# A first batch that takes its maxima straight from fp32 projections, context padded to 128 rows, and new instruction orders

## The reference

```python
xn = layernorm(x)
q, k, v = heads(xn @ Wq + bq), heads(xn @ Wk + bk), heads(xn @ Wv + bv)
y  = softmax(causal(q @ k.T / sqrt(8))) @ v                  # self attention
qc, kc, vc = heads(xn @ Wcq + bcq), heads(ctx @ Wck + bck), heads(ctx @ Wcv + bcv)
y += softmax(qc @ kc.T / sqrt(8)) @ vc                       # cross attention
x  = x + tanh(g_xattn) * (y @ Wp + bp)
# routed feed-forward, 16 experts, 4 of them per token, from 2 of 4 groups
xn = layernorm(x)
combine = route(sigmoid(xn @ router_weight.T), router_bias)  # 2.5 x normalised weights
x  = x + tanh(g_ffn) * sum_e combine[:, e] * ((silu(xn @ gate_e.T) * (xn @ up_e.T)) @ down_e.T)
```

## Time and profile before

| | |
|---|---|
| median of 3 runs | 371.14 us (369.06 to 373.66) |
| profiled execution | 365.4 us, of which the traced span is 363.7 us |
| TensorE busy | 331.4 us (91%), 3186 matmul instructions |
| VectorE busy | 258.0 us (71%) |
| ScalarE busy | 195.8 us (54%) |
| GpSimd busy | 151.6 us (42%) |
| chain that ended last | TensorE 77%, VectorE 6%, DMA 5%, SP's issuing 4% |

### The profile page before, as it was taken

One profiled execution on the slowest core, in us unless ns is written; L12 is line 12 of the kernel. 1 busy time (PEld: TensorE's weight loads), 2 busy tenths in 40 slices (PEclk: granted clock), 3 DMA queues, 4 the chain that ended last, 5 costly groups with the idle time before them and its releaser, 6 DMA issues.

```text
span 363.7 us, 8615 instructions
## 1 busy us (share of the span) xinstructions
PE 331.4 (91%) x3186; PEld 243.1 (67%) x3186; DVE 258.0 (71%) x637; ACT 195.8 (54%) x399; POOL 151.6 (42%) x174
## 2 busy tenths in 40 slices
PE   0576899989999997999999999999999999989797
PEld 0343365666677675778877778777778796766665
DVE  3423585877889889887857786977888786556751
ACT  1232156747766774576565854677457555643131
POOL 8452343304225438416750459226700280712414
PEclk9999999999999999999999999999999999999999
DMA  5474543665644564045724344417412501405000
GB/s 138 79 165 151 165 123 103 190 203 175 153 125 132 154 152 132 24 150 139 187 76 132 92 112 137 145 49 167 127 50 99 119 2 50 85 4 131 2 14 14
DMA packets 32505, 40.45 MB, mean 111 GB/s; under 512 B 3056, under 2 KB 29440, under 8 KB 29984
## 3 DMA queue, kind: packets, MB, share of 16 engines
q1 hardware_dynamic: 32464, 39.91, 41.6%
HBM read 29.84 MB, written 7.45 MB: 103 GB/s over the span
## 4 chain that ended last, share of the span: by engine, by line
PE 77%; DVE 6%; DMA 5%; SPq 4%; issue 3%; POOL 2%; ACT 2%; POOLq 0%; ACTq 0%; DVEq 0%
PE bank L818 14%; PE bank L884 13%; PE bank L777 8%; PE bank L799 8%; PE bank L905 6%; PE bank L774 6%; PE bank L796 5%; PE bank L838 2%; DMA k_stack<-part_scr 2%; DMA comb<-c_scr 2%; SPq L478 2%; PE bank L859 2%; DVE row_max L969 2%; PE bank L840 1%; PE bank L825 1%
## 5 line engine op out<-in xcount | busy, mean ns | idle before, releaser
L969 DVE TENSOR_REDUCE row_max<-bank 128x2 f32<-128x512 f32 (+1 forms) x224 | 148.2, 685 | 49.8 <-PE bank L777 32.8
L689 ACT ACTIVATE probs<-bank 128x512 f32<-128x512 f32 x224 | 127.9, 595 | 60.6 <-PE bank L799 35.3
L884 PE MATMUL bank<-xn2T,w_pairs_sb 128*128 128x256 f32 x256 | 66.4, 386 | 1.5 <-issue 1.1
L818 PE MATMUL bank<-probs,v_ext 128*32 128x256 f32 (+1 forms) x1024 | 61.8, 362 | 0.0
L613 POOL TENSOR_TENSOR f_h<-f_h,comb 128x512 f32<-128x512 f32 x32 | 40.1, 1270 | 28.9 <-ACT comb L710 12.1
L777 PE MATMUL bank<-k_stack,q_stack 72*128 72x256 bf16 x256 | 49.4, 291 | 2.5 <-DVE row_max L969 1.5
L884 PEld LDWEIGHTS bank<-xn2T,w_pairs_sb 128*128 128x128 f32 x256 | 44.0, 190 | 8.3 <-issue 3.1
L799 PE MATMUL bank<-q_stack,k_stack 73*128 73x256 bf16 x256 | 47.3, 282 | 0.3 <-ACT probs L689 0.2
L406 POOL TENSOR_TENSOR rest<-proj,part 128x512 f32<-128x512 f32 x14 | 16.2, 1155 | 68.0 <-ACT part L662 68.0
L818 PEld LDWEIGHTS bank<-probs,v_ext 128*32 128x32 f32 x1024 | 27.1, 110 | 21.9 <-issue 7.2
L774 PE MATMUL bank<-k_stack,q_stack 121*128 121x128 bf16 (+1 forms) x384 | 38.4, 229 | 2.3 <-DVE row_max L969 2.0
(11 more groups left out here) (111 smaller groups left out, 372.5 us busy)
## 6 DMA issues: line engine op xcount, KB each, us to landing
q_stack<-part_scr SPq DMA_DIRECT2D x45, 192.0 KB
k_stack<-part_scr SPq DMA_DIRECT2D x45, 192.0 KB
comb<-c_scr SPq DMA_DIRECT2D x14, 512.0 KB, 6.4
part_scr<-part SPq DMA_DIRECT2D x48, 128.0 KB, 2.2
x_in<-in_x SPq DMA_DIRECT2D x8, 128.0 KB, 2.6
w_pairs_sb<-in_w_pairs SPq DMA_DIRECT2D x1, 1024.0 KB, 8.0
out<-y_out SPq DMA_DIRECT2D x8, 128.0 KB, 2.8
q_stack<-q_stack SPq DMA_DIRECT2D x2, 384.0 KB, 5.5
```

The costliest lines, as they stand in the source:

```text
L689: nc.scalar.activation(probs[:, seq % NP, :], exp_bank[s % 2][:, :], ACT.Exp).then_inc(exp_done, 1)
L818: last = pe.matmul(pv_bank[32 * n:32 * n + VW, col + q0:col + T], v_ext[:, b % 2, kind, kt].rearrange("p h v -> p (h v)")[:, at:at + VW], ...
L884: last = pe.matmul(bank_of[:, n * T:(n + 1) * T], w[:, e0:e0 + 128], xn2T[:, :], start=True, stop=True)
L969: nc.vector.tensor_reduce(row_max[:, kind, qt, h0:h0 + nh], max_bank[k % 2][:, :].rearrange("p (h k) -> p h k", h=nh), AX.X, ALU.max).then ...
```

## The change

- The maxima of batch 0 no longer come from the stack. The weights of the four projections are copied with columns in order of heads (wh), the projections are computed a second time with them (hp), and the keys are copied four times, each time with all but every fourth head's rows multiplied by zero (hk, with of_head), the queries once (hq). Head h is then a product over a set of 32 rows (h // 4): first_max (word mxd) computes two chunks at a time, whose heads lie in different sets of 32 rows, in two PSUM banks, with the banks of the experts as the second pair. S1_CHUNKS is reordered for that. The stack of batch 0 is still made, for the exponentials; its waits move there.
- Context and its weights are padded with zeros to 128 rows by two memsets on VectorE.
- GpSimd's constants (more) and the clearing of v_ext (vclear) wait for the first normalisation; rstd1:0 stands ahead of more.
- All six orders are new. Among others: both cross splits of batches 0 and 1 are on GpSimd, which were on VectorE; batch 1's maxima follow xnT:2; SP loads batch 2 ahead of the masks, and the second half of batch 0's cross keys comes after the stores of batch 1.

```diff
-S1_CHUNKS = [(CROSS, qt, H // 2 * half + 2 * g, 2, 256) for half in range(2) for qt in range(NQ) for g in range(4)]
+S1_CHUNKS = [(CROSS, qt, H // 2 * half + 2 * g, 2, 256) for half in range(2) for qt in range(NQ) for g in (0, 2, 1, 3)]
 CROSS_C1 = len(S1_CHUNKS)
-S1_CHUNKS += [(SELF, 0, 4 * g, 4, 128) for g in range(4)] + [(SELF, 1, 2 * g, 2, 256) for g in range(8)]
+S1_CHUNKS += [(SELF, 0, 4 * g, 4, 128) for g in range(4)] + [(SELF, 1, 2 * g, 2, 256) for g in (0, 2, 1, 3, 4, 6, 5, 7)]
...
     'pe': '''
-        xnT:0 proj:0 proj:0:1 vproj:0 xnT:1 proj:1 proj:1:1 vproj:1 max:0 max:0:1 xnT:2 max:0:2 max:0:3 proj:2 max:0:4
-        max:0:5 max:0:6 max:0:7 max:0:8 max:0:9 max:0:10 proj:2:1 max:0:11 max:0:12 shift:0 max:0:13 max:0:14 max:0:15
...
+        xnT:0 colh:0 proj:0 hp:0 hp:0:1 proj:0:1 mxd:0 mxd:0:1 mxd:0:2 mxd:0:3 vproj:0 mxd:0:4 shift:0 xnT:1 proj:1
+        mxd:0:5 hp:0:2 mxd:0:6 hp:0:3 exp:0 mxd:0:7 mxd:0:8 exp:0:1 mxd:0:9 shift:0:2 exp:0:2 mxd:0:10 exp:0:3
+        proj:1:1 mxd:0:11 exp:0:4 exp:0:5 mxd:0:12 mxd:0:13 pv:0 exp:0:6 shift:0:1 exp:0:7 vproj:1 exp:0:8 exp:0:9
+        pv:0:1 xnT:2 max:1 exp:0:10 max:1:1 exp:0:11 max:1:2 proj:2 max:1:3 max:1:4 exp:0:12 max:1:5 max:1:6 exp:0:13
+        exp:0:14 max:1:7 proj:2:1 max:1:8 exp:0:15 max:1:9 pv:0:2 pv:0:3 max:1:10 exp:0:16 exp:0:17 max:1:11 max:1:12
...
     'pool': '''
-        more:0 rstd1:0 vclear:0 rstd1:1 xn1:1 sp1:0:1 sp3:0:1 rstd1:2 xn1:2 sp1:1:1 xres:0 sp3:1:1 sp1:2 sp3:2 sp1:2:1
...
+        rstd1:0 more:0 xres:0 sp1:0 sp3:0 vclear:0 rstd1:1 xn1:1 sp1:0:1 sp3:0:1 sp1:1 sp3:1 sp1:1:1 sp3:1:1 rstd1:2
...
     'sp': '''
-        load:0 w:0 load:1 tri:0 pd0:0 load:2 pd2:0 pd1:0 tri:0:1 pd0:0:1 kh:0 qh:0 kh:0:1 pd2:1 ones:0 pd1:0:1 pd2:0:1
-        pd0:1 pd1:1 qh:0:1 qst:0:1 kst:0:1 pd0:1:1 pd1:1:1 shd:0 pd2:1:1 kst:1 shd:0:2 qst:1 pd0:2:1 load:3 pd0:2
...
+        load:0 w:0 load:1 load:2 tri:0 pd1:0 pd0:0 pd2:0 ones:0 tri:0:1 kh:0 qh:0 load:3 shd:0 qh:0:1 pd1:0:1 pd0:1
+        pd1:1 pd2:0:1 pd2:1 pd0:0:1 kh:0:1 shd:0:2 kst:1 qst:1 shd:0:1 pd0:1:1 pd2:1:1 kst:0:1 pd1:1:1 qst:0:1 qst:1:1
...
-        w_ctx_sb = sb("w_ctx_sb", [CC, 2 * C])
+        w_ctx_sb = sb("w_ctx_sb", [C, 2 * C])
...
-        ctx_in = sb("ctx_in", [CC, NX, T])
+        ctx_in = sb("ctx_in", [C, NX, T])
...
+        first_banks = (max_bank, (gate_bank, up_bank))
...
             def more_constants():
+                pool.wait_ge(xn_done, 1)
...
             def clear_values():
+                pool.wait_ge(xn_done, 1)
...
+            def by_head(kind, n):
+
+                act.wait_ge(of_head_made, 3)
+                act.wait_ge(heads_ready, (2, 1)[n > 0] if kind == CROSS else 3)
+                q, k = (exp_bank[1][:, 0:T], exp_bank[0][:, 0:T]) if kind == CROSS else (pv_bank[:, T:2 * T], pv_bank[:, 0:T])
+                if n == 0:
+                    last = nc.scalar.activation(q_h[kind], q, ACT.Identity, bias=bias_qh[:, 1 - kind:2 - kind], scale=SCALE)
+                else:
+                    last = nc.scalar.activation(k_h[kind][:, n - 1], k, ACT.Identity, bias=bias_kh[:, kind, n - 1:n], scale=of_head[:, n - 1:n])
+                last.then_inc(heads_made[kind], 1)
...
+            def first_max(p):
+
+                kind = S1_CHUNKS[2 * p][0]
+                if 2 * p in (0, CROSS_C1):
+                    pe.wait_ge(heads_made[kind], 5)
+                if 2 * p == CROSS_C1:
+                    pe.wait_ge(const_made, 3)
+                ge(pe, max_taken, 2 * p - 2)
+                kind, qt, _, nh, keys = S1_CHUNKS[2 * p]
+                ps = [first_banks[p % 2][j][:, :].rearrange("p (h k) -> p h k", h=nh) for j in range(2)]
+                for n in range(nh):
+                    for j in range(2):
+                        h = S1_CHUNKS[2 * p + j][2] + n
+                        rows_of = slice(h // 4 * 32, h // 4 * 32 + 32)
+                        last = pe.matmul(ps[j][:, n, :], q_h[kind][rows_of, qt * 128:(qt + 1) * 128], k_h[kind][rows_of, h % 4, 0:keys],
+                                         start=n == 0, stop=kind == CROSS and n == nh - 1, tile_position=(h // 4 * 32, 0))
+                if kind == SELF:
+                    for j in range(2):
+                        last = pe.matmul(ps[j][:, :, keys - 128:keys], tri_q[:, 0:128], tri_k[:, 0:128].unsqueeze(1).broadcast_to([ROWS, nh, 128]),
+                                         start=False, stop=True)
+                last.then_inc(max_scores, 2)
...
+            nc.vector.memset(w_ctx_sb[CC:C, :], 0.0).then_inc(ctx_padded, 1)
+            nc.vector.memset(ctx_in[CC:C, :, :], 0.0).then_inc(ctx_padded, 1)
```

More of the change, by code:

```diff
@@ L97 @@
[L97 to L101, removed]
@@ new lines @@
+        max:2:16 exp:1:20 max:2:17 shift:2 exp:1:21 max:2:18 pv:1:4 max:2:19 exp:1:22 max:2:20 xn2T:0 exp:1:23
+        max:2:21 exp:1:24 logits:0 max:2:22 pv:1:5 y:1 exp:1:25 max:2:23 ga:0 exp:1:26 max:2:24 max:2:25 exp:1:27
+        pv:1:6 exp:2 exp:2:1 max:2:26 pv:1:7 max:2:27 exp:2:2 ga:0:1 exp:2:3 vproj:3 exp:2:4 up:0 shift:2:1 pv:2
+        exp:2:5 exp:2:6 combT:0 up:0:1 y:1:1 exp:2:7 exp:2:8 ga:0:2 max:3 max:3:1 xnT:4 up:0:2 yT:1 max:3:2 exp:2:9
+        exp:2:10 max:3:3 proj:4 exp:2:11 max:3:4 pv:2:1 exp:2:12 max:3:5 wp:1 max:3:6 exp:2:13 ga:0:3 max:3:7 up:0:3
@@ L398, in stack_here @@
             if b >= 0:
-                eng.wait_ge(stack_in[b % SLOTS][kind], STACK_DMAS[kind] * 16 * (b // SLOTS + 1))
+                none = kind == SELF and b % SLOTS == 0
+                eng.wait_ge(stack_in[b % SLOTS][kind], STACK_DMAS[kind] * 16 * (b // SLOTS + 1) - 16 * none)
         def split_step(eng, b, kind, n):
@@ L464, in load_stack @@
                     sp.dma_start(st[i * BLOCK:(i + 1) * BLOCK, b % SLOTS, kind], src).then_inc(stack_in[b % SLOTS][kind], 16)
[L465 to L466 removed]
+                if kind == SELF and qk == 0 and b > 0:
+                    if b == 1:
                         sp.wait_ge(const_step, 4)
@@ L719, in _ @@
                     project(b, n)
+                elif what == "wh":
+                    weights_by_head(n)
+                elif what == "hq":
+                    by_head(n, 0)
+                elif what == "hk":
+                    for head in range(4):
+                        by_head(n, head + 1)
                 elif what == "part0":
@@ L754, in _, with columns_by_head, project_by_head @@
             pe.wait_ge(const_made, 1)
+            def columns_by_head():
+                pe.wait_ge(w_first, 48)
+                pe.wait_ge(ident_copied, 1)
+                pe.matmul(pv_bank[:, 0:6], ident_h, cols_sb[:, :], start=True, stop=True).then_inc(cols_ready, 1)
+            def project_by_head(n):
+                if n == 0:
+                    pe.wait_ge(ctx_padded, 2)
+                    x_here(pe, 0)
+                else:
+                    misc_evacuated(pe, "xnT", 0)
+                if n == 2:
+                    pe.wait_ge(cols_taken, 1)
+                pe.wait_ge(w_copied, n + 1)
+                to = (exp_bank[0][:, 0:T], exp_bank[1][:, 0:T], pv_bank[:, 0:T], pv_bank[:, T:2 * T])[n]
+                last = pe.matmul(to, w_h[:, n], xnT[:, :] if n else ctx_in[:, 0, :], start=True, stop=True)
+                if n != 2:
+                    last.then_inc(heads_ready, 1)
@@ L783, in exp_chunk @@
                     pe.wait_ge(ones_in, 16 * SLOTS)
+                    pe.wait_ge(first_heads_in, 96)
+                elif b == 0 and s in (CROSS_C2 // 2, CROSS_C2):
+                    stack_here(pe, 0, kind)
+                if b == 0 and s == CROSS_C2:
+                    pe.wait_ge(tri_in[0], 32)
                 if b == 0 and s == 0:
@@ L806, in weigh_values @@
                     misc_evacuated(pe, "vproj", b)
+                if b == 0 and g == 0:
+                    pe.wait_ge(heads_made[SELF], 5)
                 if g4 == 0:
@@ L924, in _ @@
                     max_chunk(b, n)
+                elif what == "colh":
+                    columns_by_head()
+                elif what == "hp":
+                    project_by_head(n)
+                elif what == "mxd":
+                    first_max(n)
                 elif what == "exp":
```

308 lines of the change are left out of this document (166 added, 142 removed).

## The result

The change made the kernel slower: 374.02 us in the median (370.38 to 380.64, 20 executions) against 368.41 us for the kernel before, measured beside it (363.78 to 373.66, and one execution of 789.51). The ratio is 1.0185, with a 95% interval of [1.0147, 1.0223]. The forecast was 358 us. The profiled execution took 375.67 us, its span 373.9 us, 10.2 us more than before. TensorE is busy for 351.3 us (94%), 19.9 us more, with 3256 matmul instructions against 3186.

A forecast was written before the change was run, and what follows sets the result against it. TensorE was taken to bound the kernel from 60 us on, waiting before. Start 9.8 plus padding 3.3 gave 13.1 us off the profiled 365.4, so 352.3, or 358 in median terms; range 350 to 374.

The forecast's parts named there:

- the start: Start of the chain: normalisation 2.7 us less, rstd 1.0 us earlier, so transposes at 6.5 instead of 10.21 us.
- the price of a pair at a given level: Direct chunk pairs, taken as side by side: 1.15 to 1.6 us at the upper clock level, 2.1 to 3.0 at the lower.
- the queues: GpSimd's splits and SP's loads: batch 0's self stacks issued 41 to 46 us, landed by 50, wanted at 57, so hidden.
- Rival C: Supply: GpSimd's splits or SP's waits slip some 8 us more, making TensorE wait; price 5 us, total 363; chance 0.15.
- part 4: Start of exponentials: clock rises by 24.7 us, exp:0 at 32, exp:0:16 at 57 instead of 64.53; 9.8 us won.
- Rival B: Direct scores cost twice: one after another, or side by side with low clock until first weighing; about 369; chance 0.25.
- the column tiles: Argument against doubled direct-score cost: weighing of values in 32-column tiles already ran side by side, four at a time.
- what comes after: From exp:0:16 to the end: 2.3 us of TensorE work already done, and 3.3 us saved by context padding.
- Part 7: The other new orders: nothing shows their worth; taken as 0, bounds -4 and +4 us.
- a long wait on k_stack of batch 2: Listed sign that the forecast is wrong through late supply, seen as TensorE waiting for k_stack or xn of batch 2.
- the padding's 0.3 us: Context on 128 rows: 0.3 us for each of eleven uses after the start stage, 3.3 us; bounds 0 and 5.

The follow-up runs named there:

- e10: The changed kernel with batch 0's direct cross pairs on sets of 64 rows, two heads summed, self pairs still on 32: 369.36 us, ratio 0.9898.
- e3: The changed kernel with direct scores over all 128 rows and no tile position, four heads summed per product: 364.44 us, ratio 0.9935.
- e8: The changed kernel with bf16 pairs, full-array fillers, last cross pair before exp:0, and batch 2's stacks issued earlier on SP: 368.12 us, ratio 1.0043.
- e9: e8 with the routing of batch 7 ahead of the output of batch 6 on VectorE: 367.71 us, ratio 0.9894.
- e4: The kernel before with only context and its weights padded to 128 rows: 364.91 us, ratio 0.9982.

## Why the prediction was wrong

**Right: the start.** The transposes started at 6.38 (predicted 6.5), the normalisation took 0.60 us, the first direct scores stood at 13.53 (13.9). VectorE's row of the changed kernel, which answers to the earlier trace rows:

```profile
5.63 0.60 DVE L1174 TENSOR_SCALAR xn<-x_in,mean,rstd 128x128 f32<-128x128 f32 x2 [1.00 <-POOL rstd L592]
```

**Right: the price of a pair at a given level.** Two sets of 32 rows do work side by side: 1.0 us a pair at the upper level, where 1.15 was the lower bound, and 2.0 at the lower, where I had 2.1. Masks come on top at 0.54 us (51.09 to 51.63), within the 2.1 to 3.0. The same eight instructions one after another on 64 rows are 1.81 us (four pairs from 13.50 to the next row at 20.74 in e10). The excess of a lone pair over 1.7 us is 0.3 at the lower level (21.77 to 23.78), for which 0.4 was taken. The Trainium skill, page TensorEngine Tiling (Array Packing), Key Properties, says that changing the tiling mode drains the engine, and the trace agrees: two pairs in a row have the excess of 0.3 us once (3.71 us from 16.05 to the next row at 19.76, against 3.4), a lone pair has it for itself.

**Right: the queues.** SP issued the self stacks of batch 0 from 45.06 us on (41 to 46 predicted), and no row of TensorE between 24.83 and 74.03 waits for a stack. Rival C did not come about there.

**Wrong: the step that failed is part 4's** "TensorE is then busy for 10 us without a gap, as it was before 57.80, and I put the rise of the clock here". It rose at about 63.6, not at 24.7. The inference was from one case to another that differs in what the engine does: before 57.80 it worked on 72 and 73 rows, here on sets of 32. Even there the prediction's own rows had 8 us of dense work without a rise, and the rise right behind the first weighing, which is on 128 rows. Being busy was taken for enough. e3 and e10 show that the form of the products matters: on 64 or 128 rows, one after another, the level was kept or came back; on sets of 32 rows, side by side, it did not come back in 48 us. Whether the rows or the two tiles at once do it is open. The Trainium skill, page TensorE: Matmul & The Clock Gate, Part 1, says that sustained matmul activity brings the array to 2.4 GHz. By the rule as it is worded the rise would have been there at the latest; the stretches from 30 to 60 us, busy for 29.98 us at 0.50, speak against it for 32-row tiles, two at a time.

The price follows from the rows. exp:0 came at 34.20 instead of 32 (the terms of part 4 add up to 32.3): 2.2 us. That small miss is luck: the value projection ended at 21.77, not 24.7, since the first two pairs ran at the upper level, and from there to exp:0 it took 12.4 us, not 7.6. From there to the first weighing I had 12.4 us, and it took 57.67 - 34.20 = 23.5: seven pairs with masks 18.2 instead of 9.8, six exponential chunks 3.0 instead of 1.4, the projection 1.8 instead of 0.9, the shift 0.4 instead of 0.3. That is 11.1 us. From the first weighing to exp:0:16 it took 16.4 instead of 12.6: 3.8 us, up to 63.7 at the lower level. Together 17.1 us, which is 74.03 against 57.

**Rival B had the mechanism, and too small a price.** Its second half, "side by side with the clock low until the first weighing", is nearly what happened; the level was low from 16 us to the second weighing. It was priced at 11 us because it counted only the pairs; the lower level also doubles the time of the projections, exponentials and weighings that lie between them. "Against: the column tiles" was no argument on the level: they show tiles side by side, on 128 rows.

**Also mis-sized: what comes after.** From exp:0:16 to the end I expected 5.6 us less than before (2.3 of work done ahead, 3.3 of padding), and it took 299.9 us, against 299.2 before. So 6.3 us are missing, in two places:

```profile
94.65 1.04 PE L859 MATMUL bank<-k_stack,q_stack 72*128 72x256 bf16 x4 [1.72 <-DMA k_stack<-part_scr]
95.61 1.94 PE L907 MATMUL bank<-probs,v_ext 128*32 128x256 f32 x16
...
347.39 0.66 PE L914 MATMUL bank<-ident,xn 128*128 128x128 f32 x2 [1.99 <-DVE xn L1174]
...
349.46 4.47 PE L995 MATMUL bank<-w_down,f_h 128*128 128x128 f32 x20
```

At 94.65 TensorE waits 1.72 us for the key stack of batch 2, and from there to 101 us it runs at the lower level (a weighing 1.94 us instead of 1.00): 1.7 and about 3 us. In the tail it waits 1.99 us for the last normalisation (1.07 before), which VectorE does in 2.42 us beside two steps of GpSimd, and 20 instructions of the down projection then take 4.47 us (2.48 before); the last 32 of the kernel take 3.84, so 20 would be 2.4 at the upper level: 0.9 and about 2 us. That is 7.6 us, a little more than is missing. Part 7 had the orders at 0, between -4 and +4; the sign "a long wait on k_stack of batch 2", given for rival C, was there, but what it cost was mostly the level after it. That the new orders caused these two waits is argued, not shown: e8 removed the one and met another, and e9's change of VectorE's order left the other as it was (1.96 us).

**Right: the padding's 0.3 us.** e4's time doesn't show the saving, but the rows do. Self and context projection together take 0.43 + 0.43 us at the upper level, where the earlier trace rows have 1.16:

```profile
66.42 0.60 PE L928 MATMUL bank<-xnT,w_model_sb 128*128 128x256 f32 x2
66.85 0.59 PE L930 MATMUL bank<-ctx_in,w_ctx_sb 128*128 128x256 f32 x2
67.28 0.60 PE L859 MATMUL bank<-k_stack,q_stack 72*128 72x256 bf16 x4
```

## What to carry to other kernels

Busy is not the same as fast: read the granted clock beside the busy time, stretch by stretch, and price every operation at both levels, with everything that lies between. Before a dense stage is moved onto narrow row sets, ask which level the engine will be granted there; side by side at the lower level it may be dearer than one after another at the upper. In e10 and e3 the plainer form, 64 or 128 rows in sequence, took 1.8 us a pair and the clever one 2.0. Those two sum several heads in a product, so they are probes and no replacement as they stand.
